# A layer stack on one Trainium2 core: the diagonal bias of the row scores in attention is added by VectorE from a table instead of by matmuls

## The reference, cut to what matters

```python
scores = jnp.einsum('bqhd,bkhd->bhqk', q, k) / math.sqrt(head_dim)   # 16 heads of 16
pos = jnp.arange(L)                                                  # L = 1024
bias = -jnp.abs(pos[None, :] - pos[:, None]).astype(jnp.float32)
scores = scores + slopes[None, :, None, None] * bias[None, None]
probs = jax.nn.softmax(scores, axis=-1)
```

## Time and profile before

| | |
|---|---|
| median of 3 runs | 3318.43 us (3315.69 to 3322.08) |
| span of the profiled execution | 3314.4 us, 4.0 us under that median |
| PE busy | 3139.1 us, 95% of the span |
| VectorE busy | 2521.7 us, 76% |
| ScalarE busy | 1985.8 us, 60% |
| GpSimd busy | 780.8 us, 24% |
| attention, first to last L1639 and L1701 | about 1163 us to 2967 us of the span |

### The profile page before, as it was taken

One profiled execution on the slowest core, in us unless ns is written; L12 is line 12 of the kernel. 1 busy time (PEld: TensorE's weight loads), 2 busy tenths in 40 slices (PEclk: granted clock), 3 DMA queues, 4 the chain that ended last, 5 costly groups with the idle time before them and its releaser, 6 DMA issues. The chain is left out here.

```text
span 3314.4 us, 79004 instructions
## 1 busy us (share of the span) xinstructions
PE 3139.1 (95%) x31780; PEld 1960.7 (59%) x31780; DVE 2521.7 (76%) x4848; ACT 1985.8 (60%) x2967; POOL 780.8 (24%) x916
## 2 busy tenths in 40 slices
PE   7999999995999689999999999999999999998999
PEld 3666666663888555555555555555555555546888
DVE  6777777755888478778878788788787887837887
ACT  2544555432666317776767676767676766775665
POOL 3445454532222201111110110111111101002222
PEclk8999999986999759999999999999999999998999
DMA  1000000003111422122222131222221312202111
GB/s 54 15 15 27 27 28 27 21 15 105 52 52 51 100 39 46 25 49 47 46 50 46 25 71 25 46 50 46 50 43 27 66 30 42 42 12 95 52 58 39
DMA packets 110349, 145.51 MB, mean 44 GB/s; under 512 B 21792, under 2 KB 94256, under 8 KB 109200
## 3 DMA queue, kind: packets, MB, share of 16 engines
q1 hardware_dynamic: 108776, 136.78, 17.5%
q0 software_dynamic: 768, 2.77, 0.4%
q10 hardware_dynamic: 440, 0.90, 0.2%
HBM read 53.79 MB, written 38.24 MB: 28 GB/s over the span
## 5 line engine op out<-in xcount | busy, mean ns | idle before, releaser
L1896 DVE TENSOR_REDUCE b_half_max<-banks 128x1 f32<-128x512 f32 x2048 | 1304.3, 685 | 290.5 <-PE banks L1560 174.9
L1814 ACT ACTIVATE b_p_t<-banks 128x1024 f32<-128x1024 f32 x1024 | 1040.3, 1026 | 372.1 <-PE banks L1560 231.2
L1639 PE MATMUL banks<-b_k_stack,b_q_stack 62*128 62x512 f32 x2048 | 835.0, 480 | 26.4 <-issue 10.4
L1701 PE MATMUL banks<-b_q_stack,b_k_stack 64*128 64x512 f32 x2048 | 832.9, 469 | 8.8 <-ACT b_p_t L1814 7.7
L1655 PE MATMUL banks<-b_p_t,b_v 128*17 128x256 f32 x8192 | 628.4, 385 | 0.2 <-ACT b_p_t L1814 0.2
L1701 PEld LDWEIGHTS banks<-b_q_stack,b_k_stack 64*128 64x128 f32 x2048 | 344.4, 185 | 373.0 <-issue 322.8
L1639 PEld LDWEIGHTS banks<-b_k_stack,b_q_stack 62*128 62x128 f32 x2048 | 342.0, 188 | 75.5 <-DVE b_half_max L1896 33.9
L1560 PE MATMUL banks<-b_unit,b_tables 64*128 64x64 bf16 x4096 | 373.1, 197 | 0.0
L1137 ACT ACTIVATE ffn_relu<-banks,ffn_scale_fc 128x512 f32<-128x512 f32 x256 | 176.2, 688 | 205.3 <-PE banks L1069 205.3
L1082 PE MATMUL banks<-ffn_proj_t,ffn_r_hi 128*128 128x256 f32 x1024 | 262.2, 289 | 2.7 <-DVE ffn_r_lo L1263 2.5
L1560 PEld LDWEIGHTS banks<-b_unit,b_tables 64*128 64x128 bf16 x4096 | 186.2, 96 | 120.7 <-issue 70.6
(11 more groups left out here) (247 smaller groups left out, 4937.7 us busy)
## 6 DMA issues: line engine op xcount, KB each, us to landing
ffn_x<-x SPq DMA_DIRECT2D x32, 512.0 KB, 3.8
b_q_stack<-b_qk_hi SPq DMA_DIRECT2D x252, 64.0 KB
b_k_stack<-b_qk_hi SPq DMA_DIRECT2D x252, 64.0 KB
a_x<-hidden_states SPq DMA_DIRECT2D x16, 512.0 KB, 4.1
x<-a_x SPq DMA_DIRECT2D x16, 512.0 KB, 2.9
x<-ffn_x SPq DMA_DIRECT2D x16, 512.0 KB, 2.8
b_x<-x SPq DMA_DIRECT2D x8, 1024.0 KB, 5.5
out<-ffn_x SPq DMA_DIRECT2D x16, 512.0 KB, 2.9
```

What stands on the lines that cost most here:

```text
L1639: last = pe.matmul(m, q_stack[rows, slot, qb * P:(qb + 1) * P], k_stack[rows, slot, half * BANK:(half + 1) * BANK], start=True, stop=not h ...
L1701: last = pe.matmul(out, k_stack[stack, slot, kb * P:(kb + 1) * P], q_stack[stack, slot, half * BANK:(half + 1) * BANK], start=True, stop=n ...
L1814: act.activation(p_t[use % P_BUFS][:, :, :], scores[use % 2], ACT.Exp, scale=slopes()[pair][0]).then_inc(p_made, 1)
L1896: dve.tensor_reduce(half_max[:, (pair + rg * PAIRS) * QB + qb, half:half + 1], misc.at["max", g, turn], axis=AX.X, op=ALU.max, negate=True ...
```

## The change

The row turns lose their two L1560 matmuls. A table `near_rows` of 25 blocks of 128 columns in bf16 is kept in SBUF: four correction blocks for each of the two head pairs, with blocks of zeros around them. `near_window` picks four blocks of it so that the correction lies over the diagonal square and zeros over the rest of the bank. In the turns with `here`, VectorE's reduction is replaced by one `tensor_tensor_reduce` over 128 x 512, which adds the window to the bank, writes the sum back into the bank and gives the maximum. In the other turns the reduction stays, without its negation; the sign goes to ScalarE's copy. GpSimd loads the correction blocks of each group and pair by DMA (fp32 in memory, 256 KB, to bf16), 64 loads in all, and waits for the maxima that read the old ones. Column turns keep their matmuls. `b_v_wide` moves into a buffer that exists already, and VectorE clears the zero blocks once at the start.

The core of the diff (left out: the import, the constant, and the declarations of `near_rows` and `b_v_wide`):

```diff
@@ -82,6 +84,11 @@
     by_head = power[:, :, :, None, None] * short
     c["c_block"] = by_head.reshape(GROUPS, ROWGROUPS, GROUP // ROWGROUPS, 2, P // STACK, STACK, P).transpose(
         1, 5, 0, 2, 3, 4, 6).reshape(P, HEADS // ROWGROUPS, 2, P // STACK, P)
+    both_ways = 2 * np.minimum(0, near[None, :] - near[:, None])
+    both_ways = np.stack([both_ways, both_ways.T])
+    by_turn = power.reshape(GROUPS, ROWGROUPS, GROUP // ROWGROUPS, 1, 1, 1) * both_ways
+    by_turn = by_turn.transpose(0, 2, 4, 3, 1, 5).reshape(GROUPS, GROUP // ROWGROUPS, P, 2 * ROWGROUPS, P)
+    c["c_near_rows"] = np.stack([by_turn[:, 0], by_turn[:, 1, :, ::-1]], 1)
     c["c_unit"] = np.tile(np.eye(STACK), (ROWGROUPS, 1))
     c["c_qkscale"] = np.concatenate([np.repeat([HD ** -0.5 / unit for unit, _ in slopes()[:GROUP]], HD),
                                      np.ones(GROUP * HD)])[:, None]
@@ -1443,6 +1454,7 @@
         xn_turned, x_hi_made, x_lo_made = sem("xn_turned"), sem("x_hi_made"), sem("x_lo_made")
         v_ready, v_made = sem("v_ready"), sem("v_made")
         qk_ready, qk_hi_made, qk_made, qk_lo_made = sem("qk_ready"), sem("qk_hi_made"), sem("qk_made"), sem("qk_lo_made")
+        near_rows_in = [sem(f"near_rows_in{i}") for i in range(PAIRS)]
         row_scores, half_max_made = sem("row_scores"), sem("half_max_made")
         row_max_made, max_turned = sem("row_max_made"), sem("max_turned")
         shift_hi, shift_copied, shift_made = sem("shift_hi"), sem("shift_copied"), sem("shift_made")
@@ -1481,6 +1493,16 @@
                 g, turn = divmod(n, STEPS)
                 half, qb, pair = turn // 2 % HALVES, turn // 2 // HALVES % QB, turn // 2 // HALVES // QB
                 yield g, turn, pair, qb, half, 1 - turn % 2
+
+        def near_window(pair, qb, rg):
+
+            own, at = int(qb >= CT) * ROWGROUPS + rg, qb % CT
+            step = (NEAR if at in (1, 2) else NEAR - own) * (1 if at < 2 else -1)
+            block = NEAR + own
+            if pair:
+                block, step = NEAR_BLOCKS - 1 - block, -step
+            table = near_rows[:, block - at * step, :]
+            return AP(tensor=table.tensor, offset=table.offset, ap=[table.ap[0], [step * P, CT], [1, P]])
 
         def turns(g):
 
@@ -1631,18 +1653,14 @@
                                      ident[:, :]).then_inc(max_turned, 1)
                     if g < ALL:
                         first, slot = place(g, pair + rg * PAIRS)
-                        rows, here, at = slice(first, first + SHIFTROW), qb // CT == half, qb % CT * P
+                        rows = slice(first, first + SHIFTROW)
                         m, (used, n) = misc.take(("max", g, turn), (half_max_made, STEPS * g + turn + 1))
                         if turn % (STEPS // PAIRS) < ROWGROUPS:
                             pe.wait_ge(stacked[slot_of(g) + pair + rg * PAIRS], 112 * (g // SETS + 1))
                         pe.wait_ge(used, n)
-                        last = pe.matmul(m, q_stack[rows, slot, qb * P:(qb + 1) * P], k_stack[rows, slot, half * BANK:(half + 1) * BANK],
-                                         start=True, stop=not here, tile_position=(first, 0))
-                        if not here:
-                            last.then_inc(row_scores, 1)
+                        pe.matmul(m, q_stack[rows, slot, qb * P:(qb + 1) * P], k_stack[rows, slot, half * BANK:(half + 1) * BANK],
+                                  start=True, stop=True, tile_position=(first, 0)).then_inc(row_scores, 1)
                         yield
-                        if here:
-                            add_block_bias(m[:, at:at + P], g, pair, rg, int(qb >= CT)).then_inc(row_scores, 1)
                         yield
 
             def weigh(t, use, kb, part):
@@ -1770,7 +1788,7 @@
                         act.wait_ge(max_turned, g)
                         if g >= 2:
                             act.wait_ge(shift_made, g - 1)
-                        act.activation(shift_full[:, :], m, ACT.Copy).then_inc(shift_copied, 1)
+                        act.activation(shift_full[:, :], m, ACT.Copy, scale=-1.0).then_inc(shift_copied, 1)
                     yield
 
             def weigh(t, use, kb, part):
@@ -1888,13 +1906,19 @@
                         if g >= 2:
                             dve.wait_ge(max_turned, g - 1)
                         both = lambda i: half_max[:, :, i].unsqueeze(1).to_broadcast([P, 2, GROUP * QB])
-                        dve.tensor_tensor(row_max[:, :, :], both(0), both(1), ALU.min).then_inc(row_max_made, 1)
+                        dve.tensor_tensor(row_max[:, :, :], both(0), both(1), ALU.max).then_inc(row_max_made, 1)
                     if g < ALL:
                         if g and turn == 0:
                             dve.wait_ge(row_max_made, g)
                         dve.wait_ge(row_scores, STEPS * g + turn + 1)
-                        dve.tensor_reduce(half_max[:, (pair + rg * PAIRS) * QB + qb, half:half + 1], misc.at["max", g, turn],
-                                          axis=AX.X, op=ALU.max, negate=True).then_inc(half_max_made, 1)
+                        m, largest = misc.at["max", g, turn], half_max[:, (pair + rg * PAIRS) * QB + qb, half:half + 1]
+                        if qb // CT == half:
+                            if turn % (STEPS // PAIRS) == 0:
+                                dve.wait_ge(near_rows_in[pair], 16 * (g + 1))
+                            dve.tensor_tensor_reduce(out=m, in0=m, in1=near_window(pair, qb, rg), scale=1.0, scalar=LOWEST,
+                                                     op0=ALU.add, op1=ALU.max, accum_out=largest).then_inc(half_max_made, 1)
+                        else:
+                            dve.tensor_reduce(largest, m, axis=AX.X, op=ALU.max).then_inc(half_max_made, 1)
                     yield
 
             def weigh(t, use, kb, part):
@@ -1939,6 +1963,9 @@
             follow, finish_tails = tails(weigh, conclude)
             for v in vs:
                 dve.memset(v[:, :, :, HD:VW], 1.0)
+            dve.memset(near_rows[:, 0:NEAR, :], 0.0)
+            dve.memset(near_rows[:, 2 * NEAR:NEAR_BLOCKS - 2 * NEAR, :], 0.0)
+            dve.memset(near_rows[:, NEAR_BLOCKS - NEAR:, :], 0.0)
             dve.memset(values, 0.0).then_inc(cleared, 1)
             dve.wait_ge(ident_in, 16)
             dve.wait_ge(cleared, 1)
@@ -1946,6 +1973,13 @@
             finish_tails()
 
         def gpsimd(pool):
+            def load_near_rows(g, pair):
+                first = NEAR_BLOCKS - 2 * NEAR if pair else NEAR
+                blocks = slice(first, first + NEAR)
+                if g:
+                    pool.wait_ge(half_max_made, STEPS * (g - 1) + (pair + 1) * STEPS // PAIRS)
+                pool.dma_start(near_rows[:, blocks, :], d["c_near_rows"][g % GROUPS, pair]).then_inc(near_rows_in[pair], 16)
+
             def normalize(b):
                 x = xs[b % X_BUFS]
                 pool.wait_ge(moments, b + 1)
@@ -1974,6 +2008,8 @@
                     if (b, i) == (0, QB - 2):
                         pool.dma_start(unit[:, :], d["c_unit"]).then_inc(tables_cast, 16)
                         pool.dma_start(tables[:, :, :, :, :], d["c_block"]).then_inc(tables_cast, 16)
+                        for pair in range(PAIRS):
+                            load_near_rows(0, pair)
                     yield
                     yield
 
@@ -2002,6 +2038,10 @@
             def find_maxima():
                 lo = slice(0, GROUP * QB)
                 for g, turn, *_ in row_turns():
+                    if 0 < g < ALL and turn == TURN + 4:
+                        load_near_rows(g, PAIRS - 1)
+                    if g + 1 < ALL and turn == STEPS // PAIRS + TURN + 4:
+                        load_near_rows(g + 1, 0)
                     if g and turn == TURN + 1:
                         pool.wait_ge(shift_copied, g)
                         if g >= 2:
```

More of the change, by code:

```diff
@@ L5 @@
 from concourse import mybir
+from concourse.bass import AP
 F32 = mybir.dt.float32
@@ L23 @@
 EPS = 1e-5
+LOWEST = -3.0e38
 HEADS_A, KD, VD, LOWRANK, GATERANK, MIXES = 4, 128, 256, 32, 64, 5
```

6 lines of the change are left out of this document (5 added, 1 removed).

## The result

The changed kernel takes 3292.63 us (median of 4 runs, 3287.78 to 3295.42) against 3317.06 (4 runs, 3310.52 to 3322.08) of the kernel before: ratio 0.9918, 95% interval 0.9893 to 0.9942. It is faster by 24 us where 11 were forecast.

A forecast was written before the change was run, and what follows sets the result against it. PE was taken to set the pace, VectorE next. Terms -54 + 22 + 16 + 5 = -11 us turn the profiled 3314.4 into 3303, with 4.0 us to the median 3307 us; range 3275 to 3405.

The forecast's parts named there:

- PE's saving: Row correction matmuls gone from 492 uses: 246 at 0.14 us and 246 at 0.08 us, 54 us saved.
- X: VectorE's time from the start of the new pair (sum with maximum, short write) to the next start, assumed 0.72 us.
- rival 2: VectorE's load does not show, catching up between PE's other work suffices: -54 + 5, 3269 us; chance 0.10.
- (a) Pace: VectorE needs 1.32 us a use; without column correction PE needs 1.23; 44 us missing, half taken: +22 us.
- (b) Waits: PE's 173 waits for a maximum grow by 0.09 us each: +16 us.
- Lead: The 40 row turns of the lead that have the correction cost 0.12 us more each: +5 us.
- The slope: Each 0.01 us more on X costs the kernel about 4 us.
- rival 1: The pair runs unpipelined and VectorE becomes the bound, X 0.76 to 0.89: 3324 to 3408 us; chance 0.28.
- Covers: Zero-block clearings, at most 3.3 us, fall into VectorE's 5.21 us wait for x; table loads and GpSimd's waits cost nothing.
- ScalarE's waits for L1560: Sign of being right: ScalarE's waits for the correction matmuls, 228.2 us in the window before, shrink.
- (3): Rival: the pair's main part streams at half pace on VectorE, X about 1.26, above 3620 us; chance 0.04.

The follow-up runs named there:

- the two versions above: Kernel before with one row correction matmul instead of two: 3305.84 us; kernel before with the small matmuls grouped behind the second pair of large ones: 3347.24 us.
- plain reductions: Changed kernel with the plain reduction in every row turn, no correction in the maxima, slopes a quarter, table loads kept: 3282.47 us, 0.9901 of the kernel before.
- pairs in every turn: Changed kernel with the sum and maximum in all row turns, zeros added where the reduction stood: 3313.58 us, 0.9978 of the kernel before.
- the clearing: Changed kernel with a VectorE clearing of 32 scratch columns behind each new pair: 3300.42 us, 0.9956 of the kernel before.
- the three medians: The changed kernel measured three times, the last two without edit: 3292.63, 3292.43 and 3288.62 us; 0.9918, 0.9933 and 0.9922 of the kernel before.

## Why the prediction was right in sign and small in size

- **PE's saving, 54 us: 47.** The prices of a use were right (0.148 and 0.078 us in the median), the count was not. Uses 3, 19 and 24 of a group save 0.4, 1.3 and 0.5 us over all groups where others save 2 to 5. Uses 3 and 19 are held by ScalarE: the matmul that opens the next use waits for the exponential that frees its bank, behind use 19 never before the change and 31 times now (8.6 us), behind use 3 for 16.7 us instead of 10.4. Use 19 has no product with v and lasts only 0.6 us, so that PE comes back before an exponential of 1.03 us is done; at use 3 the exponential stands behind a copy of the projections (L1774). The end of a use 19 in the changed kernel:

```profile
2241.53 1.03 ACT L1832 ACTIVATE b_p_t<-banks 128x1024 f32<-128x1024 f32 x1 [0.19 <-PE banks L1719]
...
2242.60 0.18 PEld L1719 LDWEIGHTS banks<-b_q_stack,b_k_stack 64*128 64x128 f32 x1 [0.29 <-ACT b_p_t L1832]
```

  Use 24 saves 0.08 us in most groups and takes 0.15 more in one of four; no run shows why. I priced 492 uses alike. That the correction also costs by breaking the order is borne out by the two versions above.
- **X, 0.72: 0.63.** This is the step that failed, a term of the sum that was sized too large. I added the short part's start-to-start time to the main part's. But it starts together with the next instruction and takes no place of its own; only the main part behind it is longer, 0.73 instead of 0.69. Rather than "the row it is nearest to", L635 with 0.66, the reduction with 0.60 was nearer. With X = 0.63 my own terms give -54 + 0 + 4 + 1 = -49, rival 2's number, which did not come either.
- **(a) Pace, +22: about 1** in the changed kernel (uses 10 to 18 against plain reductions), since 2.46 us of VectorE in two uses meet 2.44 of PE. The mechanism exists: with pairs in every turn it shows, and by about half.
- **(b) Waits, +16: 10.5 to 13.6** (the changed kernel against plain reductions), near by luck. I spread 0.12 from X over 173 waits. In fact two pairs give a bank free 0.12 later than two reductions, mostly because the maximum is written 0.06 to 0.10 after a reduction's would be, and the growth sits in few places, 9.3 us of it in uses 25, 20 and 22. At use 25 this is a little over half, and VectorE's lag the rest; uses 20 and 22 were not followed up. X had to be split into two prices: 0.63 from start to start, and 0.75 to 0.79 from start to free bank.
- **Not in the prediction: +5** with plain reductions, most of it ScalarE's copies at use 9, which were hidden behind PE's correction of use 8.
- **Lead, +5: -0.5** (68.8 and 68.3 us). It grows only with more work on VectorE: 70.3 with the clearing, 71.9 with the sum in every turn.
- **The slope, 4 us for each 0.01 of X: under 2** at full clock, with the clearing, up to an X of 0.655. What rival 1 would have cost at 0.76 and more was not tried.
- **Covers.** The clearings (1.08 us, from 1125.07 on) fit in VectorE's wait for x, which shrinks from 5.21 to 4.11; the loads cost nothing; GpSimd's wait for the shift's copy is 541 us over 31 waits and never under 7.2, so the load ahead of it is never late. All as predicted. ScalarE's waits for L1560 did not shrink, against the prediction: they were the column turns'.

The sum: -47.3 in the uses with a row correction, +13.6 for the pair (11.0 at full clock), +5.4 without it, about -28.4 in the attention, against 24 to 29 us in the three medians. The forecast of -11 was off because X, and with it pace and lead, was too large; 7 us less from PE and the 5 us that were not in it partly made up for that. Of the rivals, (1) needs X above 0.75, and X is 0.63; (2), that VectorE's load does not show at all, fails by those 10.5 to 13.6 us; (3) fails at the main part's 715 ns. The Trainium skill, Vector Engine (DVE) Microarchitecture Reference, section "Points that are easy to get wrong", names the halving for two SBUF sources that are not bf16. The trace agrees as far as it goes: with one PSUM and one bf16 source, accumulator included, the main part takes 715 ns against 685 for a reduction.

Open: what makes the granted clock fall in single groups, and whether a slower VectorE brings it on; what uses 20 and 22 wait for in detail; and whether a fourth bank would take the wait at use 25 away or hand it on once more, which wasn't tried.

## What to carry to other kernels

Price an instruction that writes an accumulated value twice: from start to start for the engine's own pace, and from start to the written value for whoever waits for it. Where two engines of nearly equal pace share a short ring, count the saving only in the uses in which no other engine is due next, and look in the timeline for what the removed work was hiding, a copy on a third engine too. Here small matmuls between pairs that run side by side cost about as much by parting the pairs as by standing behind them; but grouping them delays whoever reads the result. And before two profiles are subtracted stretch by stretch, compare the granted clock of each stretch: here the whole difference between two profiles of one kernel was clock, and about half of what the clearing seemed to cost.

## What was unexpected of the hardware

The read of VectorE's accumulator (142 ns) starts in the same instant as the next main instruction, and the pair is only 0.03 us slower from start to start than a reduction of the same 512 columns, though it also reads a table and writes the bank back. A clearing of 32 columns behind it, 0.07 us long, adds 0.025 only. PE's large matmuls of two row groups lose 0.07 us when two small ones stand between the pairs (0.41 from pair to pair instead of 0.34), and behind the second pair one, two or four small ones cost the same 0.08. And one kernel's profiles hold from 5.5 to 13.7 us at the lower clock in the attention, at places that differ from profile to profile.
